# Attention on one core: VectorE's exponential in six passes, six of its blocks a unit

## The reference

```python
q = heads(xn @ q_w.T + q_b) / sqrt(16)      # 16 heads of 16 columns
k = heads(xn @ k_w.T + k_b); v = heads(xn @ v_w.T + v_b)
attn = softmax(q @ k.T)                     # 4096 x 4096 for each head
out = merge(attn @ v) @ out_w.T + out_b
ffn = bf16((fp8(xn) @ fp8(ffn_w).T) * scales + ffn_b)
result = x + out + ffn
```

## Time and profile before

| what | before |
|---|---|
| median of three executions | 1886.2 us |
| span of the profiled execution (the page gives no other time of it) | 1883.1 us |
| attention, from the first exponential's start to the last's end | 108.9 to 1840.1 us |
| ScalarE busy | 1764.1 us, 94% |
| TensorE busy | 1648.8 us, 88% |
| VectorE busy | 1552.4 us, 82% |

### The profile page before, as it was taken

How to read it: one execution, slowest core, us unless ns; L and a number is a source line. 1 busy time by engine, 2 the same in 40 slices (tenths; PEclk the granted TensorE clock), 3 DMA queues, 4 the chain that set the end, 5 groups by cost and what they waited for, 6 DMA issues and landing times.

```text
span 1883.1 us, 74604 instructions
## 1 busy us (share of the span) xinstructions
PE 1648.8 (88%) x33418; PEld 558.0 (30%) x33418; DVE 1552.4 (82%) x1908; ACT 1764.1 (94%) x1944; POOL 41.1 (2%) x57
## 2 busy tenths in 40 slices
PE   7988888888888888888888888888888888888888
PEld 4632222222222222222222222222222222222226
DVE  8687878878787888878787987878888887878786
ACT  2389999999999999999999999999999999999990
POOL 0000000000000000000000000000000000000003
PEclk9999999999999999999999999999999999999999
DMA  7420100000000100000010000001000000001003
GB/s 202 154 90 10 32 10 22 13 18 24 18 24 10 24 13 16 24 18 24 10 31 8 17 20 18 24 10 31 10 22 12 18 24 18 24 10 26 13 14 107
DMA packets 94966, 57.20 MB, mean 30 GB/s; under 512 B 55280, under 2 KB 87280, under 8 KB 94640
## 3 DMA queue, kind: packets, MB, share of 16 engines
q1 hardware_dynamic: 94160, 52.18, 10.3%
q10 hardware_dynamic: 480, 0.20, 0.0%
HBM read 30.54 MB, written 17.30 MB: 25 GB/s over the span
## 4 chain that ended last, share of the span: by engine, by line
ACT 48%; issue 37%; PE 11%; DVE 1%; POOL 1%; ACTq 1%; DMA 0%; SPq 0%; POOLq 0%; DVEq 0%
ACT probs L679 48%; PE banks L1308 3%; PE banks L1164 3%; PE banks L1267 3%; PE banks L1175 1%; ACTq L678 1%; DVE o_junk L963 1%; DVE o_sb L962 1%; POOL o_sb L600 0%; PE banks L1148 0%; POOL o_junk L600 0%; DMA qk_bias<-in_L_attn_k_b_dram 0%; DVE bits L983 0%; DVE w_max L764 0%; DVE xn_all L833 0%
## 5 line engine op out<-in xcount | busy, mean ns | idle before, releaser
L679 ACT ACTIVATE probs<-banks 128x1024 f32<-128x1024 f32 x1888 | 1731.0, 1193 | 0.3 <-PE banks L1267 0.2
L1308 PE MATMUL banks<-probs,v_st 64*32 64x512 f32 x15104 | 1004.5, 590 | 2.2
L1267 PE MATMUL banks<-q_st,k_st 50*32 50x512 f16 x16384 | 793.3, 381 | 211.9 <-ACT probs L679 208.9
L1267 PEld LDWEIGHTS banks<-q_st,k_st 50*32 50x32 f16 x16384 | 233.5, 89 | 1145.3 <-ACT probs L679 1088.8
L996 DVE SCALAR_TENSOR_TENSOR horner<-horner,bits 128x1024 f32<-128x1024 f32 x320 | 393.1, 1228 | 11.0
L1308 PEld LDWEIGHTS banks<-probs,v_st 64*32 64x32 f32 x15104 | 272.3, 106 | 66.4 <-DVE o_junk L963 11.4
L983 DVE TENSOR_SCALAR bits<-banks 128x1024 int32<-128x1024 f32 x160 | 195.9, 1225 | 76.9 <-PE banks L1267 76.8
L996 DVE SCALAR_TENSOR_TENSOR horner<-bits 128x1024 f32<-128x1024 f32 x160 | 196.1, 1226 | 5.5
L1001 DVE SCALAR_TENSOR_TENSOR d_probs<-horner,powers 128x1024 f32<-128x1024 f32 x160 | 196.0, 1225 | 5.5
L962 DVE COPY o_sb<-banks 128x512 f32<-128x512 f32 x32 | 22.1, 692 | 130.9 <-PE banks L1308 98.0
L992 DVE TENSOR_SCALAR bits<-bits 128x1024 int32<-128x1024 int32 x160 | 111.1, 694 | 5.5
(11 more groups left out here) (103 smaller groups left out, 435.6 us busy)
## 6 DMA issues: line engine op xcount, KB each, us to landing
k_st<-k_parts SPq DMA_DIRECT2D x102, 64.0 KB, 2.2
q_st<-q_parts SPq DMA_DIRECT2D x198, 32.0 KB, 1.9
k_st<-k_parts SPq DMA_DIRECT2D x102, 60.0 KB, 2.2
q_st<-neg_row SPq DMA_DIRECT2D x264, 1.0 KB, 1.7
xnT_copy<-probs SPq DMA_DIRECT2D x8, 512.0 KB, 3.1
q_parts<-x8T SPq DMA_DIRECT2D x16, 256.0 KB, 2.9
k_parts<-x8T SPq DMA_DIRECT2D x16, 256.0 KB, 2.4
w_f<-xnT_copy SPq DMA_DIRECT2D x16, 256.0 KB, 2.9
```

The source lines that it names most:

```text
L679: act.activation(probs[:, at:at + WIDE * CHUNK].rearrange("p (t c) -> p t c", t=WIDE), banks[:, bank:bank + WIDE, :], ACT.Exp, bias=EXP_SHIFT,
L1267: last = pe.matmul(banks[cols, bank + g, :], k_st[rows, keys], blocks[rows, j], start=True, stop=True, tile_position=(g * GROUP, t * VCOLS))
L1308: last = pe.matmul(banks[VCOLS * qb:VCOLS * (qb + 1), 6 + half, cols], v_st[keys, kt, :], src[keys, g * CHUNK:(g + 1) * CHUNK][:, cols], s ...
```

## The change

VectorE's exponential gets a new form. The first pass is as before, and its integer words are now used whole. One pass masks their fraction bits, as an integer, into `powers`. Three two-source passes make a quartic of that fraction from its factors, in the units of the integer, reading the masked integers directly. The last pass scales the quartic and adds it to the words, and writes the sum as an integer into `d_probs`, whose bits are the float wanted. The pass that put the fraction under the exponent of one is gone, so there are six passes, four of them counted by `D_STEPS`. The wait on `d_ready` moves ahead of the first pass of a block, as the last pass of the block in front still reads `bits`. The bias of both engines' exponentials goes from 120.8 powers of two to 127.

VectorE takes six blocks a unit, at places 10, 22, 30, 38, 46 and 54, and ScalarE 58. The sixth is the second half of key tile 30, whose first half it already had.

```diff
--- before.py
+++ after.py
@@ -34,6 +34,7 @@
 
 ROUND_TO_3_BITS = 1.5 * 2.0 ** 20
 EXPONENT_BITS = 0x7F800000
+FRACTION = 2.0 ** 23
 PARTS = 2
 Q_TERMS = (0, 0, 1)
 K_TERMS = (0, 1, 0)
@@ -49,11 +50,13 @@
 QK_SCALE = 2.0 ** 10
 SMALLEST_BOUND = 16.0
 LOG2E = 1.4426950408889634
-ONE_BITS = 0x3F800000
 MANTISSA_BITS = 0x007FFFFF
-EXP_BIAS = 1013270912.0
-EXP_SHIFT = -EXP_BIAS / 2.0 ** 23 / LOG2E
-POLY = (-0.1511656492948532, 12.309608459472656, 23.089841842651367, 37.712982177734375)
+EXP_BIAS = 127.0
+EXP_SHIFT = -EXP_BIAS / LOG2E
+CURVE_ROOT = -1.00001524 * FRACTION
+CURVE_SLOPE = 5.89161538 * FRACTION
+CURVE_BASE = 22.8639511 * FRACTION ** 2
+CURVE_SCALE = 0.0134250815 * FRACTION ** -3
 WIDE = 2
 BUFS = 3
 RING = 16
@@ -83,10 +86,10 @@
     ROW_LOADS = 16 * PARTS * QB
     ALL_ROW_LOADS = 16 * GROUPS * PARTS * BLOCKS
     PAIRS = KT * QB // WIDE
-    D_AT = (9, 23, 33, 43, 53)
+    D_AT = (10, 22, 30, 38, 46, 54)
     MAX_AT = 19
-    D_PAIRS = ((KT // 2 - 1, 0), (KT // 2 - 1, 1), (KT - 1, 0), (KT - 1, 1), (KT - 2, 0))
-    D_STEPS = 5
+    D_PAIRS = ((KT // 2 - 1, 0), (KT // 2 - 1, 1), (KT - 1, 0), (KT - 1, 1), (KT - 2, 0), (KT - 2, 1))
+    D_STEPS = 4
     D_BLOCKS = len(D_PAIRS)
     HALF = 2 * CHUNK
     AE = PAIRS - D_BLOCKS
@@ -95,7 +98,7 @@
     SAMPLED = VCOLS
     KEY_TILES = P // VCOLS
     SCALE = float(DH) ** -0.5
-    UNIT = LOG2E * 2.0 ** 23
+    UNIT = LOG2E * FRACTION
     NORM = float(D) ** 0.5
     TO_EXP = SCALE / QK_SCALE
     NH1 = HEADS + 1
@@ -976,31 +979,31 @@
                     steps = h * (UNITS * D_BLOCKS * D_STEPS) + (u * D_BLOCKS + n) * D_STEPS
                     at = u * c.places + D_AT[n]
                     bank = take_bank(h, at)
-                    words, tops = bits.bitcast(I32), powers.bitcast(I32)
+                    words, fraction = bits.bitcast(I32), powers.bitcast(I32)
+                    to = slice(n % 2 * HALF, (n % 2 + 1) * HALF)
                     if n:
-                        dve.wait_ge(c.d_chain, steps)
+                        dve.wait_ge(c.d_ready, done)
                     dve.wait_ge(c.st_done, h * c.head_places + (at + 1))
                     dve.tensor_scalar(words.rearrange("p (t c) -> p t c", t=WIDE), banks[:, bank:bank + WIDE, :],
                                       to_bits[:, 0:1] if c.full else UNIT * TO_EXP, 0.0, ALU.mult, ALU.max
                                       ).then_inc(c.d_taken, 1)
                     dve.wait_ge(c.d_taken, taken_at(h, u, D_AT[n]))
-                    if n:
-                        dve.wait_ge(c.d_ready, done)
-                    dve.tensor_scalar(tops[:, :], words[:, :], EXPONENT_BITS, None, ALU.bitwise_and
+                    dve.tensor_scalar(fraction[:, :], words[:, :], MANTISSA_BITS, None, ALU.bitwise_and
                                       ).then_inc(c.d_chain, 1)
                     dve.wait_ge(c.d_chain, steps + 1)
-                    dve.tensor_scalar(words[:, :], words[:, :], MANTISSA_BITS, ONE_BITS, ALU.bitwise_and,
-                                      ALU.bitwise_or).then_inc(c.d_chain, 1)
-                    for j in range(3):
-                        dve.wait_ge(c.d_chain, steps + (2 + j))
-                        dve.scalar_tensor_tensor(out=horner[:, :], in0=(horner if j else bits)[:, :], scalar=POLY[j],
-                                                 in1=bits[:, :], op0=ALU.add, op1=ALU.mult).then_inc(c.d_chain, 1)
+                    dve.scalar_tensor_tensor(out=horner[:, :], in0=fraction[:, :], scalar=CURVE_ROOT,
+                                             in1=fraction[:, :], op0=ALU.add, op1=ALU.mult).then_inc(c.d_chain, 1)
+                    dve.wait_ge(c.d_chain, steps + 2)
+                    dve.scalar_tensor_tensor(out=powers[:, :], in0=fraction[:, :], scalar=CURVE_SLOPE,
+                                             in1=horner[:, :], op0=ALU.mult, op1=ALU.add).then_inc(c.d_chain, 1)
+                    dve.wait_ge(c.d_chain, steps + 3)
+                    dve.scalar_tensor_tensor(out=horner[:, :], in0=powers[:, :], scalar=CURVE_BASE,
+                                             in1=horner[:, :], op0=ALU.add, op1=ALU.mult).then_inc(c.d_chain, 1)
                     dve.wait_ge(c.d_chain, steps + D_STEPS)
                     if n >= 2:
                         dve.wait_ge(c.pv_done, h * STEPS + (PV_0 + u * KT + c.sum_at[D_PAIRS[n - 2][0]] + 1))
-                    dve.scalar_tensor_tensor(out=d_probs[:, n % 2 * HALF:(n % 2 + 1) * HALF], in0=horner[:, :],
-                                             scalar=POLY[3], in1=powers[:, :], op0=ALU.add, op1=ALU.mult
-                                             ).then_inc(c.d_ready, 1)
+                    dve.scalar_tensor_tensor(out=d_probs.bitcast(I32)[:, to], in0=horner[:, :], scalar=CURVE_SCALE,
+                                             in1=words[:, :], op0=ALU.mult, op1=ALU.add).then_inc(c.d_ready, 1)
 
                 def normalise(h, u, link0):
```

## The result

The changed kernel takes 1923.5 us, the median of four executions (1923.2 to 1924.3), against 1886.4 on the same chip: a ratio of 1.020 (95% interval 1.019 to 1.022), **37.2 us slower**. Forecast were 1930 us, slower, with a range of 1913 to 1948.

What follows compares the result with a forecast made beforehand. ScalarE's exponentials were taken as the bound before, VectorE's late blocks after: 1.36 us more a unit, 43.5 us over 32 units, on the 1883.1 us trace plus 3.1 us gave 1930 us, slower, range 1913 to 1948.

Steps and rivals of the forecast that it cites:

- The sign and the mechanism: Attention units: slower, as VectorE needs 7.02 us a block where its places give 6.43, and frees banks late.
- The shorter block: VectorE's exponential: dropping a 0.694 us pass and its gap takes a block from 7.72 to 6.99 us.
- the sentence on the wait: VectorE's first pass waiting for the last pass in front: claimed to cost no more than the gap, 0.03 to 0.04 us.
- The sum: One unit: 55.44 us against 54.08, from -0.905, +0.10, +0.26 and +1.91; 43.5 us over 32 units.
- The rest of the unit: A unit outside exponentials 23 to 57: 25.98 us, with 0.36 at block 1 and 0.18 carried unexplained.
- the 1.91 for late banks: Exponentials 23 to 57: ScalarE waits 1.91 us a unit for banks VectorE frees late, 29.46 us against 27.55.
- the slack: Three bank pairs at block 2: up to 1.09 us of VectorE's lateness is free; each 0.1 us is 3.2 us in total.
- The range's ends: Total time, 1913 to 1948 us: slack 15 us down; up, the quantising collision and half of the dearer integer passes.
- Block 1 near the maxima: Place 22, three behind the maxima: exponential 23 starts 0.36 us late instead of 0.10, so +0.26 a unit.
- The margin at the sums: Every second unit, between the quantising's end and taking the sums: 0.9 us remain, so TensorE isn't held.
- The prediction's rival: The quantising runs into the sums, holding TensorE every other unit: half a microsecond missing costs 8 us, 1938 us; 5%.
- The faster rival: Attention units: ScalarE stays the bound, 53.53 us a unit, 1869 us; no change at a block of 6.65 us; 6%.

Runs made afterwards that it cites:

- e6: Changed kernel with the third two-source pass on 752 of its 1024 columns: 1887.4 us against 1887.8, ratio 1.000.
- e2: Kernel before, with its seven-pass exponential, given six blocks at the change's places: 2003.9 us, ratio 1.063.
- e3: Changed kernel without the third of its four two-source passes: 1864.4 us, ratio 0.989.
- e5: Changed kernel with two tiles of integer words in turn, so a block's first pass needn't wait for the last pass in front: 1908.5 us, ratio 1.011.
- e12: e7 with the quantising of x cut from six passes to one scaling: 1865.9 us, ratio 0.990.
- e4: Changed kernel with blocks at 9, 21, 30, 39, 48, 56 and the maxima at place 17: 1858.6 us, ratio 0.986.
- e10: Changed kernel with only the maxima moved, from place 19 to 17: 1905.7 us, ratio 1.011.
- e7: Changed kernel with blocks at 10, 22, 31, 40, 49, 57, the maxima still at 19: 1901.7 us, ratio 1.008.
- e11: Kernel before, with its seven-pass exponential, given six blocks and the maxima at e4's places: 1963.6 us, ratio 1.041.

## Why the prediction was right

**The sign and the mechanism** were right, and for the reasons given. ScalarE waits for banks at VectorE's pace; the idle time stands at exponentials 41, 49 and 57; VectorE's blocks 2 to 5 have no idle time ahead; TensorE has the new wait. e6, the changed kernel and e2 are on one line: 54.14, 55.25 and 57.7 us a unit for 6.74, 7.02 and 7.63 us from block to block, four to one. e3, with a block quick enough to wait for scores, is at the floor of these places, 53.43, where 53.53 was forecast.

**The shorter block**: 6.99 us forecast, and 901.69 to 908.64 is 6.95, with a first pass of 1.18 in this one (1.22 in most). 7.02 from block to block is exact.

**The step that failed** is the sentence on the wait: "That wait costs no more than the gap, VectorE being in order." It costs 0.11 to 0.12 us a block, 0.47 a unit (55.25 to 54.78 in e5), 15 us. The sum didn't suffer, since I had added a gap to a block's length and so had the pace with the wait; what I had wrong is the pace without it. In the trace of before no block stood right behind another, but it did show the overlap elsewhere, between the last pass of the quantising and an addition that waits for nothing of it. Timeline of VectorE in the kernel before, which I had not used:

```profile
974.37 0.43 DVE L728 TENSOR_SCALAR x8T<-horner 128x512 bf16<-128x512 f32 x1
974.71 0.69 DVE L1048 TENSOR_TENSOR x_all<-x_all,bo_sb 128x512 f32<-128x512 f32 x1
```

The addition starts at 974.71, ahead of 974.37 + 0.43 = 974.80.

**The sum**: 55.44 a unit forecast, 55.25 measured. From exponential 23 to 57 it was 29.46 against 29.32 (902.18 to 931.50). The same habit made part of it: block 1 starts at 901.69, before the maxima's last instruction ends (901.56 + 0.21 = 901.77), and not 0.04 behind it, so 0.12 sooner. The rest of the unit was 25.98 against 25.93. So the 1.91 for late banks was mis-sized by 0.14: exponential 33, for which I had 0.16 us of delay, starts at 910.44, 8.26 behind exponential 23 where its own pace gives 8.25. Block 2 was some 1.1 late, at the edge of the slack. The range's ends don't follow exactly from the terms named: 15 down is 1915, and 8 and half of 27 up is 1951. The result lies inside either pair.

**Block 1 near the maxima**, forecast at 0.26 a unit: e12 against the mean of e4's two kinds of unit gives 53.43 - 53.17 = 0.26. That it fits so well is in part luck, since e4's blocks also stand elsewhere and e12 quantises less. In the changed kernel, where VectorE's lateness starts there too, taking the maxima away is worth 0.56 (e10).

**The margin at the sums**: 0.9 us forecast ahead of taking the sums in the units with the quantising. VectorE in such a unit of the changed kernel (last pass, end of quantising, first instruction on the sums):

```profile
990.76 1.23 DVE L1005 SCALAR_TENSOR_TENSOR d_probs<-horner,bits 128x1024 int32<-128x1024 f32 x1
...
995.33 0.68 DVE L1051 TENSOR_TENSOR x_all<-x_all,bo_sb 128x512 f32<-128x512 f32 x1
996.94 0.69 DVE L965 COPY o_sb<-banks 128x512 f32<-128x512 f32 x1 [0.93 <-DVE x_all L1051]
```

0.93 us of idle time. The margin was right, and e7 shows what happens without it. The prediction's rival counted what is missing as lost, half a microsecond for half; e7's wait of 1.6 us costs 0.9 us in a unit at full clock, but 2.5 us in the 14 in which the granted clock fell behind it. The rival had no term for the clock.

**The faster rival** needed a block under 6.65 us to be no loss. With 6.72 a block, e6 lasts 54.14 us a unit against 54.08, so by four to one the point of no change is near 6.70, 0.05 above the forecast. The Trainium skill's table (VectorE: DVE Perf Modes, section "The TRN2 errata — SBUF-src ops pay a fixed extra latency per instruction"), 58 cycles and the elements, gives an estimate of 1.13 us a two-source pass, and by it this rival. The trace after doesn't agree, with 1.225 us on integers as on floats.

## What to carry to other kernels

When work is moved off the bounding engine, compare the interval between two pieces of it at their places with the time that one takes, not the engine's busy share: VectorE had some 7 us free a unit (48.3 busy of 55.25) and was late all the same, and with nine places between blocks, the same work gained 27 us. Where it can't keep up, the loss per round is the number of intervals in a row times the shortfall, less the slack that the buffers give once. After spacing the work out, look at what comes behind the last piece: the first such layout (e7) only moved the wait to the sum banks. And price such a wait on TensorE with its clock: a wait of 1.6 us cost 0.9 us at full clock and 2.5 where the granted clock fell after it.

## What the runs showed of the hardware

- A VectorE instruction that waits for nothing of the one in front starts ahead of its end: 0.07 us ahead in e2 (713.72 against 713.79) and 0.09 in e5 (909.02 against 907.88 + 1.23 = 909.11), where one that waits for it starts 0.03 to 0.04 behind. Over the 128 steps from block to block in which VectorE set the pace (four a unit) that was 15 us.
- The length that the profile gives an exponential depends on what stands in front of it: 1193 ns in the mean before, 1090 in the changed kernel, where many start after idle time or follow one that did. One that starts after idle time is given 1.02 us (917.46 in the changed kernel), and the ones behind it a little more each, up to 1.08 (922.89). From start to start it is 0.905 us in both, so the length is no price.
- VectorE's two-source passes cost 1225 to 1226 ns on 1024 columns with integers on either source or at the output, and 0.94 us on 752 columns.
- TensorE's granted clock fell from 1.00 to 0.50 (2.4 to 1.2 GHz) for 3.41 us behind a wait of 1.6 us for the sum banks, in 14 of e7's 15 units with that wait; in e11, with waits of 1.8 to 1.9 us, in 14 of 15, for 3.4 or 6.8 us. It didn't in one unit of each. Neither the changed kernel nor e12, without that wait, shows such a fall from the first unit's block 0 to the last's.
